# Expert loop of a fused attention and expert layer: gate matmuls of 32 rows in two row groups, and one 1024-column gelu for blocks 2 and 3

## The reference

```python
z = jnp.einsum('nd,sdr->nsr', xf, P)              # 8 slots, 16 wide
scores = jnp.einsum('nsr,smr->nsm', z, C)         # 64 experts per slot
topv, topi = jax.lax.top_k(scores, 4)
w = jax.nn.softmax(topv, axis=-1)
h = jax.nn.gelu(jnp.einsum('nsr,nskrh->nskh', z, W1g) + b1g)   # hidden 32
yl = jnp.einsum('nskh,nskhr->nskr', h, W2g) + b2g
comb = jnp.einsum('nskr,nsk->nsr', yl, w)
out = jax.nn.gelu(comb.reshape(n, 128) @ G1 + g1b) @ G2 + g2b
```

## Time and profile before

| what | us |
|---|---|
| median of 3 runs | 971.04 (970.57 to 973.81) |
| the profiled execution | 974.09 |
| its span, first to last instruction | 972.3 |
| PE busy in it | 899.8 (93%) |
| DVE busy | 671.3 (69%) |
| ACT busy | 593.7 (61%) |
| POOL busy | 477.6 (49%) |

### The profile page before, as it was taken

One profiled execution on the slowest core, in us unless ns is written; L12 is line 12 of the kernel. 1 busy time (PEld: TensorE's weight loads), 2 busy tenths in 40 slices (PEclk: granted clock), 3 DMA queues, 4 the chain that ended last, 5 costly groups with the idle time before them and its releaser, 6 DMA issues.

```text
span 972.3 us, 16073 instructions
## 1 busy us (share of the span) xinstructions
PE 899.8 (93%) x5394; PEld 417.3 (43%) x5394; DVE 671.3 (69%) x1670; ACT 593.7 (61%) x870; POOL 477.6 (49%) x446
## 2 busy tenths in 40 slices
PE   3599999999999978799999999999999999999997
PEld 1267777777777756222222322322232223222322
DVE  4346555666666667677777888787777877876764
ACT  0221211125332245688888889898889888987774
POOL 0133434233335525477755666556556655664442
PEclk8699999999999977799999999999999999999999
DMA  9300001000000176766778787879788878888672
GB/s 269 118 1 1 1 2 69 2 1 1 1 1 15 30 129 97 227 204 213 220 221 248 229 243 239 249 226 247 213 250 232 254 208 243 235 246 276 231 235 97
DMA packets 87212, 151.32 MB, mean 156 GB/s; under 512 B 30083, under 2 KB 54276, under 8 KB 86481
## 3 DMA queue, kind: packets, MB, share of 16 engines
q1 hardware_dynamic: 86158, 147.04, 50.8%
q10 hardware_dynamic: 972, 3.24, 2.6%
HBM read 135.99 MB, written 14.25 MB: 155 GB/s over the span
## 4 chain that ended last, share of the span: by engine, by line
PE 78%; ACT 10%; DVE 5%; issue 2%; DMA 1%; SPq 1%; POOL 1%; ACTq 0%; DVEq 0%; POOLq 0%
PE ps L760 17%; PE ps L699 14%; PE ps L737 8%; PE ps L422 8%; PE ps L430 5%; PE ps L489 4%; PE ps L481 3%; PE ps L498 3%; PE ps L539 2%; PE ps L459 2%; ACT ring L1057 2%; PE ps L511 2%; ACT L939 2%; DVE ring L1494 1%; ACT ring L1064 1%
## 5 line engine op out<-in xcount | busy, mean ns | idle before, releaser
L1696 POOL TENSOR_TENSOR ring<-ring,wbc 128x512 f32<-128x512 f32 x192 | 244.7, 1279 | 170.4 <-ACT ring L1064 162.4
L1494 DVE TENSOR_TENSOR ring<-ps,ring 128x1024 f32<-128x1024 f32 x192 | 235.0, 1224 | 109.4 <-PE ps L737 80.1
L699 PE MATMUL ps<-zst,w1st 99*128 99x512 bf16 x768 | 216.0, 388 | 18.0 <-ACT ring L1057 14.2
L760 PE MATMUL ps<-ring,w2cur 128*32 128x512 f32 x1536 | 205.6, 608 | 0.0
L1057 ACT ACTIVATE ring<-ps 128x1024 f32<-128x1024 f32 x192 | 197.2, 1027 | 6.4 <-PE ps L699 6.1
L1551 POOL TENSOR_TENSOR t<-t 128x768 f32<-128x768 f32 x48 | 87.4, 1832 | 204.4 <-DVE t L1185 204.4
L1066 ACT ACTIVATE ps<-ps 128x512 f32<-128x512 f32 x192 | 113.9, 593 | 59.2 <-PE ps L699 59.2
L699 PEld LDWEIGHTS ps<-zst,w1st 99*128 99x128 bf16 x768 | 72.0, 98 | 156.5 <-ACT ring L1057 34.6
L1497 DVE TENSOR_TENSOR ring<-ps,wbc 128x512 f32<-128x512 f32 x192 | 130.5, 680 | 1.4 <-DMA wbc<-w_rows 1.4
L737 PE MATMUL ps<-wst,sel 96*128 96x512 bf16 x384 | 119.0, 392 | 6.3 <-DVE ring L1494 5.4
L1183 DVE TENSOR_TENSOR t<-ps,rope 128x768 f32<-128x768 f32 x48 | 45.7, 952 | 110.1 <-PE ps L430 73.9
(11 more groups left out here) (166 smaller groups left out, 1149.5 us busy)
## 6 DMA issues: line engine op xcount, KB each, us to landing
wbc<-w_rows SPq DMA_DIRECT2D x192, 512.0 KB, 5.2
w2cur<-in_w SPq DMA_DIRECT2D x48, 256.0 KB, 4.6
w_parts<-wp SPq DMA_DIRECT2D x72, 64.0 KB, 3.3
zst<-z_parts SPq DMA_DIRECT2D x72, 64.0 KB, 5.1
wst<-w_parts SPq DMA_DIRECT2D x72, 64.0 KB, 4.6
w1st<-w_parts ACTq DMA_DIRECT2D x12, 256.0 KB
z_parts<-zp SPq DMA_DIRECT2D x6, 384.0 KB, 5.2
out_h<-h SPq DMA_DIRECT2D x12, 192.0 KB, 4.5
```

The costliest lines, as they stand in the source:

```text
L699: return pe.matmul(bank(to), w1st[0:99, 4 * a + j, col:col + P], zst[0:99, (i // 2) % 2, j, :], start=True, stop=True)
L760: mm = pe.matmul(bank(YBANK, 0, 512, 32 * j, 32 * j + 32), w2cur[:, n, j, :], ring[:, (4 * g + j) % RING, :], start=False, stop=(n == 7 an ...
L1494: dve.tensor_tensor(v, ps[:, WBANK * 512:WBANK * 512 + 1024], v, ALU.mult).then_inc(s["duo_done"], 1)
L1696: pool.tensor_tensor(ring[:, slot, :], ring[:, slot, :], wbc[:, g % 4, 1, :], ALU.mult).then_inc(s["tri_done"], 1)
```

## The change

- *Row groups.* The gate matmul's 96 rows (32 experts x 3 parts) become 32 rows (8 experts x 3 parts and a fourth of zeros). The 32 experts of an i lie in four groups of 32 partitions of `wst`; for block 0 the group is n // 2, and block 1's half of `wst` is loaded turned by one group, so that the two matmuls of a pass read different row groups. `sel` becomes 128 x 2 x 128, stored as bf16 in the input, and needs no cast. `w_parts` gets a fourth part, filled with zeros by one DMA early on, and its order is that of the load.
- *One gelu for blocks 2 and 3.* TBANK and PBANK change places, so that blocks 2 and 3 lie in neighbouring banks, and one gelu of 1024 columns writes both to `ring`. Both first-layer matmuls (`pair_firsts`) now stand behind the gates in PE's order and wait for `pair_gelu` of the pass before.
- *The products.* DVE's product of block 2 reads `ring` instead of PSUM; POOL's of block 3 waits for `pair_gelu` instead of `tri_gelu`.
- *The entry.* The scores of tile 5 and their copy follow the first matmuls and gelus instead of leading them.

```diff
-JBANK, PBANK, TBANK, WBANK, YBANK = 2, 3, 4, 5, 7
+JBANK, TBANK, PBANK, WBANK, YBANK = 2, 3, 4, 5, 7
-    w_parts = nc.dram_tensor("w_parts", (3, S * M // 2, B * T), BF16, kind="Internal").ap()
+    w_parts = nc.dram_tensor("w_parts", (2, 2, 2, 4, 8, 4, B * T), BF16, kind="Internal").ap()
...
-            sel = alloc(region, "sel", [96, 8, P], BF16)
-            sel_f = ring[0:96, 0:2, :]
+            sel = alloc(region, "sel", [P, 2, P], BF16)
...
+            sp.dma_start(w_parts[:, :, :, :, :, 3, :].rearrange("a j t r m n -> (a j t r m) n").bitcast(F32),
+                         t["zeros"].to_broadcast([S * M // 2, B * T // 2])).then_inc(s["zeroed"], 16)
...
-                for k in range(3):
-                    row = w_parts[k, a * P:a * P + P, blk * BLK:blk * BLK + BLK]
-                    sp.dma_start(wst[32 * k:32 * k + 32, i % 2, :, :],
-                                 row.rearrange("(j e m) n -> e m j n", j=2, e=2)[kt]).then_inc(s["wst_ld"], 16)
+                v = [w_parts[a, j, kt, :, :, :, blk * BLK:blk * BLK + BLK].rearrange("r m k n -> (r m k) n") for j in range(2)]
+                sp.dma_start(wst[:, i % 2, 0, :], v[0]).then_inc(s["wst_ld"], 16)
+                sp.dma_start(wst[32:P, i % 2, 1, :], v[1][0:96, :]).then_inc(s["wst_ld"], 16)
+                sp.dma_start(wst[0:32, i % 2, 1, :], v[1][96:P, :]).then_inc(s["wst_ld"], 16)
...
-            def tri_first(g):
+            def pair_firsts(g):
 
                 if g > 0:
-                    pe.wait_ge(s["tri_gelu"], g)
-                else:
-                    pe.wait_ge(s["res"], PAIRS - 1)
-                first(g, 3).then_inc(s["tri_full"], 1)
-
-            def two_first(g):
-
-                if g > 0:
-                    pe.wait_ge(s["two_done"], g)
-                first(g, 2).then_inc(s["two_full"], 1)
+                    pe.wait_ge(s["pair_gelu"], g)
+                first(g, 2)
+                first(g, 3).then_inc(s["pair_full"], 1)
...
-                    mm = pe.matmul(bank(WBANK + j), sel[:, n, :], wst[0:96, i % 2, j, :], start=True, stop=True)
+                    q = 32 * ((n // 2 + j) % 4)
+                    mm = pe.matmul(bank(WBANK + j), sel[q:q + 32, n % 2, :], wst[q:q + 32, i % 2, j, :],
+                                   start=True, stop=True)
...
-            scores(LEAD, PBANK)
-            duo_firsts(0)
-            duo_gates(0)
-            tri_first(0)
-            two_first(0)
+            duo_firsts(0)
+            pair_firsts(0)
+            pe.wait_ge(s["res"], PAIRS - 1)
+            scores(LEAD, PBANK)
+            duo_gates(0)
...
                     duo_firsts(g + 1)
-                    tri_first(g + 1)
...
                     duo_gates(g + 1)
-                    two_first(g + 1)
+                    pair_firsts(g + 1)
...
-            act.wait_ge(s["ld_sel"], 16)
-            act.copy(sel[:, :, :].rearrange("p q n -> p (q n)"), sel_f.rearrange("p a n -> p (a n)")).then_inc(s["sel_cast"], 1)
...
-                act.wait_ge(s["tri_full"], g + 1)
-                act.activation(ring[:, slot + 3, :], bank(TBANK), ACT.Gelu_apprx_tanh).then_inc(s["tri_gelu"], 1)
-                act.wait_ge(s["two_full"], g + 1)
-                act.activation(bank(JBANK), bank(JBANK), ACT.Gelu_apprx_tanh).then_inc(s["two_gelu"], 1)
+                act.wait_ge(s["pair_full"], g + 1)
+                act.activation(ring[:, slot + 2:slot + 4, :].rearrange("p a n -> p (a n)"),
+                               ps[:, JBANK * 512:JBANK * 512 + 2 * BLK], ACT.Gelu_apprx_tanh).then_inc(s["pair_gelu"], 1)
+                if g == 0:
+                    copy_scores(LEAD, PBANK)
...
-                dve.wait_ge(s["two_gelu"], g + 1)
+                dve.wait_ge(s["pair_gelu"], g + 1)
                 dve.wait_ge(s[f"spread{g % 4}"], 16 * (g // 4 + 1))
-                dve.tensor_tensor(ring[:, slot + 2, :], bank(JBANK), wbc[:, g % 4, 0, :],
+                dve.tensor_tensor(ring[:, slot + 2, :], ring[:, slot + 2, :], wbc[:, g % 4, 0, :],
                                   ALU.mult).then_inc(s["two_done"], 1)
...
-                pool.wait_ge(s["tri_gelu"], g + 1)
+                pool.wait_ge(s["pair_gelu"], g + 1)
                 pool.wait_ge(s[f"spread{g % 4}"], 16 * (g // 4 + 1))
```

More of the change, by code:

```diff
@@ L184, in fused_layer @@
                  "w_stored r_stored zst_ld wst_ld spread0 spread1 spread2 spread3 w2_lo w2_hi s_full s_copied t_full wT_done "
-                 "t_top t_mr p_dist e_done n_done p_em p_w hi_done r_done mid_done lo_done sel_cast "
-                 "duo_full duo_gelu duo_w duo_done two_full two_gelu two_done tri_full tri_gelu tri_done "
+                 "t_top t_mr p_dist e_done n_done p_em p_w hi_done r_done mid_done lo_done "
+                 "duo_full duo_gelu duo_w duo_done pair_full pair_gelu two_done tri_done "
                  "second_done y_kept u_full u_done o_full "
@@ L281, in store_gates @@
                 for k in range(3):
-                    sp.dma_start(w_parts[k, :, tile * P:tile * P + P].rearrange("(g p) n -> p g n", p=P),
+                    sp.dma_start(w_parts[:, :, :, :, :, k, tile * P:tile * P + P].rearrange("g j t r m n -> (j t r m) g n"),
                                  wp[:, k, :, :]).then_inc(s["w_stored"], 16)
@@ L288, in load_z @@
                 if m >= 2:
[L289 removed]
+                    sp.wait_ge(s["pair_full"], 16 * (m - 1))
                 if a == 0:
@@ L343, in _ @@
             sp.wait_ge(s["wo_s"], PAIRS // 2)
-            sp.dma_start(sel_f, t["sel"]).then_inc(s["ld_sel"], 16)
+            sp.dma_start(sel[:, :, :].rearrange("p q n -> p (q n)").bitcast(F32), t["sel"]).then_inc(s["ld_sel"], 16)
             for dst, src in ((b2w[:, :, :], t["b2"]), (g1[:, :, :], t["g1"]), (g1b[:, 0:1], t["g1b"]), (g2[:, :], t["g2"])):
@@ L355, in _ @@
             load_z(0)
+            sp.wait_ge(s["zeroed"], 16)
             load_gates(0)
@@ L689, in _ @@
             pe.wait_ge(s["x2_e"], 6)
-            pe.wait_ge(s["sel_cast"], 1)
+            pe.wait_ge(s["ld_sel"], 16)
             pe.wait_ge(s["ld_late"], 16 * 5)
@@ L1048, in final_gelu @@
                                bias=g1b[:, 0:1]).then_inc(s["u_done"], 1)
-            act.wait_ge(s["sel_cast"], 1)
-            copy_scores(LEAD, PBANK)
             for g in range(GROUPS):
@@ L1748, in constants @@
     vsc = (gamma[None, :] ** -pos[:, None]).reshape(CH, P, H).transpose(1, 0, 2)
-    sel = np.zeros((3, 32, 8, 4, HID))
-    for m in range(32):
-        sel[:, m, m // 4, m % 4, :] = 1
+    sel = np.zeros((4, 32, 2, 4, HID), np.uint16)
+    for m in range(8):
+        sel[:, 4 * m:4 * m + 3, m // 4, m % 4, :] = 0x3F80
     halves = np.kron(np.eye(2), np.ones((DV, DV))) / DV
@@ L1755, in constants @@
             "causal": np.triu(np.ones((P, P))).astype(f), "ident": np.eye(P, dtype=f),
-            "sel": sel.reshape(96, 2, BLK).astype(f), "halves": halves.astype(f),
-            "iota_p": np.arange(P, dtype=f)[:, None], "iota_x": np.tile(np.arange(IMG, dtype=f), (P, 1)),
+            "sel": sel.reshape(P, 2 * P).view(f), "halves": halves.astype(f),
+            "zeros": np.zeros((1, B * T // 2), f), "iota_p": np.arange(P, dtype=f)[:, None], "iota_x": np.tile(np.arange(IMG, dtype=f), (P, 1)),
             "ones": np.full((3, 2048), 0x3F803F80, dtype=np.uint32).view(f)}
```

3 lines of the change are left out of this document (1 added, 2 removed).

## The result

The changed kernel takes 1011.38 us, median of 4 runs (1010.25 to 1018.9); on the same chip the ratio to the kernel before is 1.0426 (95% interval 1.0372 to 1.048). The profiled execution took 1011.41, its span is 1009.6, 37.3 more than before. The page of the changed kernel: span, busy time by engine, the chain by engine, and the groups of the loop (columns as in the groups of before: busy us, mean ns | idle before).

A forecast was written before the change was run, and what follows sets the result against it. PE was taken to bound the kernel, 78% of the chain, with little lead. Losses of 35, 10.5 and 4.5 us total 50: 974.1 + 50 - 3 = 1021 us (1003 to 1038, chance 0.62); 8-in-10 range 957 to 1048.

The forecast's parts named there:

- Row groups: 0.09 us saved, pass 2.31: Gate matmuls on PE: side by side they save 0.215 us less 0.12 for switching out, making PE's iteration 2.31.
- The collision: the loser stands still, DVE ends 0.55 behind POOL: DVE's block-2 and POOL's block-3 products, both from SBUF: one waits; DVE coming second ends 0.55 us behind POOL's.
- ACT's gain of 0.17 is off the chain: Joint gelu of blocks 2 and 3: ACT gains 0.17 us an iteration, off the chain outside the exponentials.
- The tile i = 12, forecast 25.5: One tile with routing, stepped through: intervals of 10.24, 5.66 and 9.56 us, 25.5 in all for 22.5.
- It keeps itself up: POOL is always first: Expert loop: the pair's gelu is always ready about 0.5 us before DVE, so POOL goes first; 2.54 us an iteration.
- The last five tiles: Tiles at the end: 32 intervals of 2.40 us lose 0.14 each, 4.5 us.
- the rival of 959: DVE comes first in most iterations, or operands don't collide; PE rules and the time falls to 959; chance 0.14.
- the twelve plain tiles: Tiles with routing but neither z projections nor output matmuls: 12 x 2.9 = 35 us lost.
- The rival of 996: In the loop, PE's own pauses put DVE ahead again, so blocked time is half, 50/2: 996; chance 0.08.
- Seven tiles with other PE work, forecast 10.5: Tiles with z projections (three) or output matmuls (four): only the last three intervals pay, 7 x 1.5 = 10.5 us.
- Nothing, with its cover: Entry, bank swap, larger loads, zero fill cost nothing; an occasional wait on `wbc` loads costs a microsecond or two.
- The clock, a rival: PE's idle time may bring half clock behind the exponentials in every tile: about 1.2 us x 19 = 23, 1044; chance 0.12.

The follow-up runs named there:

- the kernel with next to no collisions (0.9989): The changed kernel without POOL's product of block 3 and with DVE's copy of the top four written as a reduction: 970.94 us, ratio 0.9989 to the kernel before.
- its like with two gelus (0.9886): The kernel before with only the gate matmuls changed to 32 rows in two row groups: 959.23 us, ratio 0.9886.
- narrow_block3_behind_gates: The kernel before with the row groups alone, plus block 3's first-layer matmul moved from ahead of the second layer to behind the gates: 966.0 us, 0.9943.

## Why the prediction was right, and where it was not

The forecast of 1021 was 10 us too high; the side, the mechanism and most of the sizes held. Held against the trace by its own steps:

- **Row groups: 0.09 us saved, pass 2.31.** Measured 0.32 + 0.97 for 0.54 + 0.86: 0.11 saved, 2.29. The pair costs one stream and the way out 0.11 (0.12 assumed). That the step alone would be worth 11 us wasn't asked; it is the one good part of the diff.
- **The collision: the loser stands still, DVE ends 0.55 behind POOL.** Measured 0.55, whatever the start. Right. But no step had the copy of the top four: 0.18 us before, it takes 0.50 in the median tile of the changed kernel, up to 0.67, beside POOL's product or its smaller work:

```profile
L1328 DVE COPY top<-top x24: 180/500/668, 283.4 to 867.3; 128x32 f32<-128x32 f32 x24
```

- **ACT's gain of 0.17 is off the chain.** Right: ACT's busy time falls and the kernel with next to no collisions (0.9989) is slower than its like with two gelus (0.9886). But "PE's order changes with it" was told and not priced: 5.5 us in narrow_block3_behind_gates, most of them in two tiles with a clock fall.
- **The tile i = 12, forecast 25.5.** DVE's 1024-column products in the changed kernel:

```profile
713.17 1.22 DVE L1487 TENSOR_TENSOR ring<-ps,ring 128x1024 f32<-128x1024 f32 x1
715.66 1.20 DVE L1487 TENSOR_TENSOR ring<-ps,ring 128x1024 f32<-128x1024 f32 x1
717.99 1.21 DVE L1487 TENSOR_TENSOR ring<-ps,ring 128x1024 f32<-128x1024 f32 x1
721.13 1.21 DVE L1487 TENSOR_TENSOR ring<-ps,ring 128x1024 f32<-128x1024 f32 x1
723.06 1.21 DVE L1487 TENSOR_TENSOR ring<-ps,ring 128x1024 f32<-128x1024 f32 x1
729.14 1.23 DVE L1487 TENSOR_TENSOR ring<-ps,ring 128x1024 f32<-128x1024 f32 x1 [1.24 <-ACT ring L1049]
...
738.27 1.22 DVE L1487 TENSOR_TENSOR ring<-ps,ring 128x1024 f32<-128x1024 f32 x1
```

  The first four intervals are 2.49 + 2.33 + 3.14 + 1.93 = 9.89 (10.24 forecast, 9.19 in the earlier trace rows), then 6.08 (5.66; 5.24), then 9.13 (9.56; 8.10): 25.10 for 25.5 and 22.53. Of the first four the second is the one that failed: 2.33, not 2.70, because there DVE came first. The 6.08 and 9.13 hold a clock fall; in the like tiles i = 14 and 15, without one, these read 5.66, as forecast, and 9.5.
- **"It keeps itself up: POOL is always first", the step that failed.** It entered in two places. The last five tiles were to lose 0.14 in each of 32 passes, 4.5 us. They lost 0.3 in all, and that only through one wait on a `wbc` load: tiles 22 and 23 are 1.0 and 0.9 us shorter than before. The joint gelu isn't ready before DVE there: ACT has a gap of 0.34 to 0.35 us ahead of it, as PE's first layer comes late (the row below, from ACT's timeline), so DVE has ended its product and, quicker to wake by 0.05, is first. The order of the two engines was set by who was busy when the common signal came, and the step took ACT's gelus to stand back to back when PE's place in the loop keeps them apart. It is the mechanism of the rival of 959 ("at 2.31 the gelus aren't back to back"), and DVE kept its 0.69 in 35 of the last 40 passes, and in 53 of the 152 before them. That is the second place: the twelve plain tiles lost 23.5 us, not 35, on average 2.0 each for 2.9. The rival of 996, in which PE's own pauses put DVE ahead again, named this too; it had half of the 50 come, and 37.3 came.
```profile
982.82 1.02 ACT L1056 ACTIVATE ring<-ps 128x1024 f32<-128x1024 f32 x1 [0.34 <-PE ps L701]
```

- **Seven tiles with other PE work, forecast 10.5.** Measured 7.3 for the four with output matmuls and 3.2 for the three with z: 10.5. That the total fits is partly luck: 1.5 was forecast for each, 1.8 and 1.1 were lost.
- **Nothing, with its cover.** Nearly so. A long wait on a `wbc` load shows once, in tile 19, which with it, and with the half clock behind it, is 2.75 us longer than before:

```profile
907.13 0.69 DVE L1490 TENSOR_TENSOR ring<-ring,wbc 128x512 f32<-128x512 f32 x1 [3.62 <-DMA wbc<-w_rows]
```

  which the prediction had as "a microsecond or two". Behind the loop 3.0 us were lost that no step had. 1.6 of them: the first output matmuls of the last block ran at a low clock (last section). The other 1.4: the last second-layer matmuls waited for POOL's last product, which had come second to DVE's and took 1.78 us.

```profile
997.27 1.06 PE L757 MATMUL ps<-ring,w2cur 128*32 128x512 f32 x8 [1.20 <-POOL ring L1689]
```

- **The sum.** 23.5 + 7.3 + 3.2 + 0.3 + 3.0 = 37.3 us between the two spans, for 50 forecast. The forecast time took off 3 us by which the profiled execution of before was slow; so 12.7 too many here are 10 too many there.
- **The clock, a rival.** Its condition came true, its price did not. Behind the exponentials the clock falls in more tiles than before, as in tile i = 12: first the stretch, with busy times, clock 0.58 (in the earlier trace rows 0.50), then L751, of the same shapes as L757 (1.07 at full clock), in PE's timeline:

```profile
722.20:725.60 3.40, 3.21 (x16) 0.82 (x20) 2.76 (x4) 1.80 (x2) 1.10 (x2) 0.58 0.94 331
```

```profile
723.68 1.94 PE L751 MATMUL ps<-wT_odd,b2w 128*32 128x512 f32 x8
```

  In all, PE's clock stood at half for 34.3 us of the span behind 410 us in the changed kernel, for 13.5 before, mostly 3.4 us at a time. It fell in five plain tiles (i = 6, 8, 10, 12, 16), and they take 25.06 to 25.14 us, where i = 14 and 15 without a fall take 25.06 and 25.05. Tiles i = 12 and i = 14, columns as in the earlier trace rows:

```profile
713.17:738.27 25.10, 21.92 (x122) 5.69 (x126) 20.14 (x48) 19.66 (x22) 16.19 (x14) 0.93 0.70 213
765.51:790.57 25.06, 21.22 (x126) 5.33 (x126) 22.18 (x48) 20.20 (x23) 16.15 (x16) 1.00 0.81 237
```

  What the slow stretch costs, the intervals behind it give back: 6.08 for 5.66, then 9.13 for 9.5. So of the 23.5 us in the plain tiles next to nothing is the clock's, in this execution. Another, of 1018.9 us, ran at a mean granted clock of 0.944, the rest at 0.953 to 0.961; it has no trace. Before, where PE leads, i = 11 and 15 with a fall took 24.39 and 24.15 us, and i = 7 without one 22.76. What brings a fall isn't shown: in each of the five tiles a pause of PE of 1.77 to 1.79 us stood up to 3 us ahead of it, and in i = 14 the same pause (1.78, before 774.74) brought none.

## What to carry to other kernels

Before moving an operand from PSUM to SBUF, look what GpSimd does at that moment: here a VectorE product with two SBUF inputs, and even a tiny f32 copy, stood still until GpSimd's product was over, and what was queued behind it on VectorE paid. Time parts of a change by themselves: here one part was worth -1.1% and the others +5.4%, and the sum hid it. When two engines are started by one signal, the order between them is set by what each still does when it comes; step the whole loop, with the gaps of the engine that signals, before calling one of them "always first". And when two versions differ by half a per cent, compare them stretch by stretch with the granted clock beside: a few clock falls can be most of the difference.

## What the runs showed of the hardware

- A 128x32 f32 copy on DVE, 0.18 us alone, took up to 0.84 beside POOL's product and up to 0.89 beside its other work; a reduction over an axis of length one writes the same values in 0.19, never stretched.
- Of two products from SBUF, one waits for all of the other. Starting 0.11 us or more behind POOL, DVE waited and ended 0.546 to 0.554 us behind it. Starting 0.04 to 0.05 us ahead, and in three passes from 0.01 ahead to 0.04 behind, DVE kept its 0.67 to 0.69, and POOL's took 1.75 to 1.84 for 1.28.
- Two 32-row matmuls in different row groups took 0.32 us, in one group 0.53, and the whole-height matmuls behind them 0.11 more than behind 96-row ones, in both cases.
- Behind a pause of 0.69 us on PE at the end of the loop, the four output matmuls L766 ran at a granted clock near half and took 3.55 us; in the kernel before, behind a pause of 0.70 us, they took 1.93. In the changed kernel another pause, of 1.20 us, stood ahead of that one, in the kernel before none; whether it brought the fall, no run tells. The timeline of PE, and the stretch with its clock:

```profile
999.03 3.55 PE L766 MATMUL ps<-ysum,g 128*64 128x512 f32 x4 [0.69 <-ACT ysum L1033]
```

```profile
999.20:1003.00 3.80, 3.38 (x4) 0.48 (x3) 0.00 (x0) 0.34 (x1) 0.00 (x0) 0.55 0.00 0
```

- The same 3.4 us at half clock cost a tile 0.0 to 0.1 us in the changed kernel, 1.4 to 1.6 in the kernel before and 1.6 to 2.9 in narrow_block3_behind_gates, each against a tile without a fall.
